# Turning normalised FFN tokens with a DMA transpose on SyncE's queue in place of TensorE transposes

## The reference, cut to what matters

```
x = x + _L0_ffn_ref(_layernorm(x, axis=-1), W_up, W_gate, W_down)

def _L0_ffn_ref(x, W_up, W_gate, W_down):
    wu, wg, wd = ternary_quant(W_up), ternary_quant(W_gate), ternary_quant(W_down)
    up = jnp.einsum('bsd,ed->bse', x, wu)        # D = 512, FF = 2048
    gate = jnp.einsum('bsd,ed->bse', x, wg)
    hidden = jax.nn.silu(up) * gate
    return jnp.einsum('bse,de->bsd', hidden, wd)
```

## Time and profile before

| what | value |
|---|---|
| median of 3 executions | 768.12 us (767.45 to 768.91) |
| span of the profiled execution, first to last instruction | 762.1 us |
| what lies around the span, by the median | 6.0 us |
| PE busy over the span | 718.1 us, 94% |
| DVE / ACT / POOL busy | 51% / 36% / 14% |
| mean granted TensorE clock | 0.983 |

### The profile page before, as it was taken

The page is one execution under the profiler, slowest core; times in us unless marked ns, Lnnn a source line. Parts: engine busy times, 40 slices in busy tenths (PEclk is TensorE's granted clock), DMA queues, the critical chain, the costliest instruction groups (busy, mean ns, idle before and its releaser), DMA issues.

```text
span 762.1 us, 11832 instructions
## 1 busy us (share of the span) xinstructions
PE 718.1 (94%) x3882; PEld 380.7 (50%) x3883; DVE 388.6 (51%) x672; ACT 276.1 (36%) x430; POOL 108.5 (14%) x154
## 2 busy tenths in 40 slices
PE   4999999999996789999994999999999999999997
PEld 2465556566464556555553444444444444444443
DVE  5568666676537855444457343453434434343223
ACT  3465554555454355222224222222222222222221
POOL 4203034033021400000005000000000000000000
PEclk9999999999998999999997999999999999999999
DMA  7983034033044396222212000020000100010001
GB/s 223 391 320 143 1 127 151 0 129 147 1 173 159 130 342 232 78 91 83 83 42 70 27 15 14 14 71 14 15 0 14 69 14 14 0 55 1 0 0 55
DMA packets 32493, 66.73 MB, mean 88 GB/s; under 512 B 6352, under 2 KB 6352, under 8 KB 31440
## 3 DMA queue, kind: packets, MB, share of 16 engines
q1 hardware_dynamic: 28464, 53.24, 20.1%
q0 software_dynamic: 4000, 13.11, 5.0%
HBM read 47.73 MB, written 18.61 MB: 87 GB/s over the span
## 4 chain that ended last, share of the span: by engine, by line
PE 85%; DVE 5%; DMA 3%; issue 2%; ACT 2%; POOL 2%; SPq 1%; DVEq 0%; POOLq 0%; ACTq 0%
PE bank L1056 31%; PE bank L1314 29%; PE bank L1324 14%; PE bank L1049 6%; PE bank L1199 2%; PE bank L1213 1%; DMA nrm<-in_L_ffn_W_down_dram 1%; PE bank L1234 1%; DMA stage<-in_L_attn_Wv_dram 1%; DVE w_att L843 1%; DVE w_att L842 1%; SPq L183 1%; POOL rs L305 1%; DVE st L568 1%; DMA n<-sorted_outputs,pos_now 0%
## 5 line engine op out<-in xcount | busy, mean ns | idle before, releaser
L1314 PE MATMUL bank<-w_att,region 128*128 128x512 f16 (+1 forms) x1024 | 233.1, 381 | 0.8 <-ACT w_att L535 0.8
L1314 PEld LDWEIGHTS bank<-w_att,region 128*128 (+1 forms) x1024 | 100.5, 98 | 120.5 <-issue 3.6
L1022 DVE SCALAR_TENSOR_TENSOR tmp<-tmp,hk,bank 128x512 f32<-128x512 f32 x64 | 47.8, 747 | 153.7 <-PE bank L1314 153.3
L1324 PE MATMUL bank<-region,tmpA 128*128 (+1 forms) x504 | 119.1, 379 | 0.0
L1056 PE MATMUL bank<-w_moe,tmpA 128*128 x456 | 104.6, 379 | 1.5 <-DVE tmpA L913 1.5
L1056 PE MATMUL bank<-xT,w_att 128*128 128x512 f16 x384 | 88.6, 387 | 4.3 <-DVE region L753 2.3
L543 ACT ACTIVATE tmp<-bank,qs 128x512 f32<-128x512 f32 x64 | 44.0, 688 | 125.1 <-PE bank L1314 125.1
L547 ACT ACTIVATE tmpA<-tmp 128x512 f16<-128x512 f32 x64 | 40.4, 631 | 121.7 <-DVE tmp L1022 121.7
L1324 PEld LDWEIGHTS bank<-region,tmpA 128*128 128x128 f16 x504 | 49.2, 98 | 59.6 <-DVE stage L1005 0.9
L1056 PEld LDWEIGHTS bank<-w_moe,tmpA 128*128 128x128 f16 x456 | 44.4, 98 | 47.1 <-issue 1.7
L1025 DVE TENSOR_TENSOR tmpA<-tmp,tmpA 128x512 f16<-128x512 f32 x64 | 44.3, 692 | 45.7 <-ACT tmpA L547 45.7
(11 more groups left out here) (134 smaller groups left out, 752.4 us busy)
## 6 DMA issues: line engine op xcount, KB each, us to landing
stage<-in_L_ffn_W_up_dram SPq DMA_DIRECT2D x8, 1024.0 KB
stage<-in_L_ffn_W_gate_dram SPq DMA_DIRECT2D x8, 1024.0 KB, 7.0
sorted_tokens<-a SPq DMA_DIRECT2D x10, 512.0 KB, 10.3
n<-sorted_tokens SPq DMA_DIRECT2D x20, 256.0 KB, 2.6
stage<-in_ctx_dram SPq DMA_DIRECT2D x4, 1024.0 KB
stage<-in_L_ffn_W_down_dram SPq DMA_DIRECT2D x4, 1024.0 KB
nrm<-in_L_ffn_W_down_dram SPq DMA_DIRECT2D x4, 1024.0 KB, 7.4
out_dram<-stage SPq DMA_DIRECT2D x16, 256.0 KB, 2.1
```

The source lines that it names most:

```text
L1022: dve.scalar_tensor_tensor(out=h32, in0=sil, scalar=hk[:, 0:1], in1=gate_ps[:, :], op0=ALU.mult, op1=ALU.mult).then_inc(s["hid_mul"], 1)
L1314: mm = pe.matmul(dst, w[:, bass.ds(cf_c, 1), k * P:(k + 1) * P].rearrange("p a n -> p (a n)"), x3T[:, bass.ds(b, 1), i, k].rearrange("p a ...
L1324: mm = pe.matmul(ffy_ps[t][:, :], hid[:, parity, i, t * P:(t + 1) * P], tern[2][:, bass.ds(c, 1)].rearrange("p a n -> p (a n)"), start=(st ...
```

## The change

For batches 1 to 3 the tile is no longer turned by PE. ACT and DVE split the normalised tile into its two fp16 halves as it lies, tokens on partitions, into `x3h`, a buffer of 128 x 1024 fp16 that takes the place of `nrm[:, 1]`, which is free by then. One DMA transpose on SP's queue for each tile then turns both halves at once, SBUF to SBUF, 256 KB, into `x3T`. PE's wait at the start of a batch is on these DMAs. SP's order of work is written out: the four transposes of batch 1, then the stores of a batch and the transposes of the batch two later. The next tile's split waits until the DMA before it has read `x3h`. Batch 0 stays as it was.

```
+    x3h = nrm[:, 1].bitcast(F16).rearrange("p (i d) -> p i d", i=2)
...
-        with sp.Fori(0, B) as b:
+        def x3_turned(b):
+            for t in range(T):
+                sp.wait_ge(s["x3_lo"], T * b + t + 1)
+                sp.dma_start_transpose(
+                    out=x3T[:, bass.ds(b, 1), :, :, t * P:(t + 1) * P].rearrange("p a i k s -> p (a i k) s"),
+                    in_=x3h.rearrange("p i d -> p (i d)")).then_inc(s["x3_in"], 16)
+
+        def stored(b):
             for t in range(T):
                 sp.wait_ge(s["out_made"], T * b + t + 1)
                 sp.dma_start(out_v[:, bass.ds(T * b + t, 1)].rearrange("p a d -> p (a d)"), out_slot[t]).then_inc(
                     s[f"out_done{t}"], 16)
+
+        x3_turned(1)
+        with sp.Fori(0, B - 2) as b:
+            stored(b)
+            x3_turned(b + 2)
+        stored(B - 2)
+        stored(B - 1)
...
+        def x3_hi_rows(i):
+            act.wait_ge(s["x3_norm"], i + 1)
+            act.wait_ge(s["x3_in"], 16 * (i - T))
+            act.activation(x3h[:, 0], nrm[:, 0], ACT.Copy).then_inc(s["x3_hi"], 1)
...
                 if nxt and cc == 2:
-                    x3_hi(b + 1, t)
+                    x3_hi_rows(T * (b + 1) + t)
...
+        def x3_lo_rows(i):
+            dve.wait_ge(s["x3_hi"], i + 1)
+            dve.tensor_tensor(x3h[:, 1], nrm[:, 0], x3h[:, 0], ALU.subtract).then_inc(s["x3_lo"], 1)
...
         def x3_normalise(b, t):
             i = T * b + t
             dve.wait_ge(s["rs3"], 2 * (i - T) + 2)
-            dve.wait_ge(s["t3_mm"], i)
+            dve.wait_ge(s["x3_lo"], i)
+            dve.wait_ge(s["t3_mm"], T)
...
                 if nxt and cc == 2:
-                    x3_lo(b + 1, t)
+                    x3_lo_rows(T * (b + 1) + t)
...
-                if nxt and cc == 1:
-                    x3_transpose((b + 1) * T + t, 0, t3_ps)
...
             if not first:
-                pe.wait_ge(s["x3_lo"], T * b + T)
+                pe.wait_ge(s["x3_in"], 16 * T * b)
```

More of the change, by code:

```diff
@@ L145, in decoder @@
     z_ps, y_ps, tx_ps, th_ps, q_ps = ps[0], ps[1], ps[2], ps[3], ps[4:8]
-    ffy_ps, up_ps, gate_ps, t3_ps = ps[0:4], ps[4], ps[5], ps[6]
+    ffy_ps, up_ps, gate_ps = ps[0:4], ps[4], ps[5]
     names = """x_first0 x_first1 x_first2 x_first3 x_rest cols_in rows_in tok_in att_in0 att_in1 att_in2
@@ L159, in decoder @@
         tx_mm xs_hi xs_lo z_mm z_act h_mul th_mm h_hi h_lo y_mm y_evac sign_a sign_b unit_mm unit_copy
-        y_added x3_stat x3_aggr x3_norm t3_mm x3_hi x3_lo pos3_copied
+        y_added x3_stat x3_aggr x3_norm t3_mm x3_hi x3_lo x3_in pos3_copied
         up_mm gate_mm up_act hid_mul hid_hi hid_lo down_mm down_last out_made""".split()
@@ L530, in _, with x3_hi @@
             unit_copies(3, j)
[L533 to L536, removed]
+        def x3_hi(t, bank):
+            act.wait_ge(s["t3_mm"], t + 1)
+            act.activation(x3T[:, 0, 0, :, t * P:(t + 1) * P], bank[:, :].rearrange("p (k s) -> p k s", k=K),
+                           ACT.Copy).then_inc(s["x3_hi"], 1)
+        def x3_hi_rows(i):
+            act.wait_ge(s["x3_norm"], i + 1)
+            act.wait_ge(s["x3_in"], 16 * (i - T))
+            act.activation(x3h[:, 0], nrm[:, 0], ACT.Copy).then_inc(s["x3_hi"], 1)
         def group(b, t, first, nxt):
@@ L548, in group @@
                 if nxt and cc == 2:
-                    x3_hi(b + 1, t)
+                    x3_hi_rows(T * (b + 1) + t)
         for t in range(T):
-            x3_hi(0, t, ps[t])
+            x3_hi(t, ps[t])
         def batch3(b, first, nxt):
@@ L931, in _, with x3_lo @@
         signs_of(3, 2)
[L934 to L938, removed]
+        def x3_lo(t, bank):
+            dve.wait_ge(s["x3_hi"], t + 1)
+            hi, lo = (x3T[:, 0, i, :, t * P:(t + 1) * P] for i in range(2))
             dve.tensor_tensor(lo, bank[:, :].rearrange("p (k s) -> p k s", k=K), hi, ALU.subtract).then_inc(s["x3_lo"], 1)
+        def x3_lo_rows(i):
+            dve.wait_ge(s["x3_hi"], i + 1)
+            dve.tensor_tensor(x3h[:, 1], nrm[:, 0], x3h[:, 0], ALU.subtract).then_inc(s["x3_lo"], 1)
         def sum3(t):
@@ L975, in _ @@
         for t in range(T):
-            x3_lo(0, t, ps[t])
+            x3_lo(t, ps[t])
         def x3_sum(b, t):
@@ L1299, in _, with x3_transpose @@
             unit_transposes(3, j)
[L1302 to L1305, removed]
+        def x3_transpose(t, bank):
+            pe.wait_ge(s["x3_norm"], t + 1)
             transposes(bank, lambda k: nrm[:, t, k * P:(k + 1) * P]).then_inc(s["t3_mm"], 1)
@@ L1346, in group @@
                     down(cf - 1, c - 1, (cc - 1) % 2, begins and cc == 1, False)
-                if nxt and cc == 1:
-                    x3_transpose((b + 1) * T + t, 0, t3_ps)
         for t in range(T):
-            x3_transpose(t, t, ps[t])
+            x3_transpose(t, ps[t])
         pe.wait_ge(s["unit_copy"], 12 * T)
```

## The result

The changed kernel runs in 761.35 us, the median of six executions (760.32 to 762.63), against 767.79 for six of the kernel before: ratio 0.9934, 95% interval 0.9913 to 0.9954. It is faster by 0.66%; the two medians alone, 6.4 us apart, would make a ratio of 0.9916, which lies inside the interval. The forecast was 770.9 us, slower by 0.36%, with a range from 762.8 to 790.0: sign and range both missed. What came true is the rival "hidden, or nearly", which had 0.38.

A forecast was written before the change was run, and what follows sets the result against it. PE was taken as the bound, without gaps in the FFN stage. Removing transposes gave -5.3 us, three boundary waits of 6.0 - 3.3 us gave +8.1, together +2.8: 770.9 us against the median of 768.12, range 762.8 to 790.

The forecast's parts named there:

- hidden, or nearly: Rival at the starts of batches 1 to 3: the transfer takes under 4.6 us, kernel faster, 762.8 us if fully covered; chance 0.38.
- the price of the turned transfer: DMA transpose of one 256 KB tile on SP's queue: 6.0 us from issue to landing, range 2.1 to 10.4.
- the three boundary terms: At the starts of batches 1 to 3, PE waits d - 3.3 us each; 8.1 us in all at d = 6.0.
- the cover: From last low half to PE's first load of the next batch: 3.53 us, 3.3 left for the transfer after issue and wake.
- What is removed: FFN stage, batches 1 to 3: 12 sets of four PE transposes at 0.44 us each, 5.3 us off the chain.
- What is changed at nothing: Split in the FFN stage: ACT's cast from SBUF 0.05 us longer, DVE's low half 0.69 us, new waits delaying nobody.
- SP's queue: Transposes placed ahead of and behind the result stores: a few us more in the queue cost nothing, late stores not missed.
- The sum's form: Whole change: -5.3 us plus three times the landing time beyond 3.3 us; +2.8 us at 6.0, break-even at 5.1.
- When a stall takes the clock: Rival at batch starts: landing 7.3 us or more, stall over 4 us, about 3 us of work lost each; chance 0.17.
- My forecast's own case: At batch starts, PE late by 1.3 to 4 us each, landing 4.6 to 7.3 us, time 766.6 to 774.8 us; chance 0.40.
- What lies around the span: Outside the profiled span of the whole kernel: 6.0 us added to the 764.9 us span to give the forecast time.
- the hidden case: At batch starts, landing within 3.3 us, so no PE wait and 5.3 us gained: 762.8 us, the range's low end.

## Why the prediction was wrong

The step that failed is **the price of the turned transfer**. I took d = 6.0 us from issue to landing, because the tokens' load (4.8 us) and 1.9 us for the bytes seemed the nearest rows, and kept 2.1 as the floor. It is 3.0. The loads of tokens and columns move single 4-byte elements at the start of the kernel, with megabytes of other loads in flight; the transpose goes in 256-byte pieces through idle DMA engines. Which of the two differences makes those loads slower was not tried. The rows nearer to it were the ones that I used as floor and as an argument for the rival: the store of as many bytes (2.1) and above all the gather (3.4). The same DMA view of before also has 20 plain loads of 256 KB on SP's queue (`n<-sorted_tokens`) that land after 2.6 us, which the earlier trace rows leave out. Turning as such adds 0.1 us to a copy of the same pieces.

With d = 3.0 in the prediction's own sum, d - 3.3 is below zero, the three boundary terms vanish and -5.3 us is left. The size was wrong, and with it the sign; that the transfer counts only by what it exceeds the cover was right.

- **What is removed**: right. 12 x 0.44 = 5.3 forecast; putting the transposes back lengthens the stage from 324.9 (324.6 where nothing is turned) to 329.8 us and brings the time back to that of before.
- **What is changed at nothing**: right. ACT 0.61 us, DVE 0.68, and what follows them starts as before. That the new wait of ACT costs nothing follows from the transfers' 3.0 us in a distance of 20.7.
- **The cover**: right in kind, small in size. 3.3 us forecast; SP issues 0.03 to 0.13 us after the low half instead of 0.17, and 3.6 to 3.7 us are there. With d of 3.9 us PE stood for 0.16 us, with 4.5 for 0.7.
- **SP's queue**: right. The stores still land after 2.1 us, and no engine waited for them.
- **The sum's form** held where it was tried. A wait is the landing less the cover: 2.4 to 2.7 us forecast for four transposes a tile and 2.31 to 2.71 measured, 4.7 forecast for the split in cc = 3 and 4.30 to 5.26 measured. The waits and the slower matmuls behind them give the longer stage within 0.3 us in three versions. No single transfer of 6 us was tried; the late landings were made with more issues or a later split.
- **When a stall takes the clock**: I had it from 4 us on. At 4.3 us and more it did each time, by 1.5 to 2.7 us for a stall, where I had put 3; but it also did after 2.31 us, in one case of three of about that length. My forecast's own case could have cost more than the +2.8 us that I gave it, as the four transposes a tile did: the sum had no term for the clock below d = 7.3.
- **What lies around the span** was not 6.0 us. In all executions that have both, time and span differ by 1.6 to 1.7 us. By that, the profiled execution of before took about 763.8 us (an estimate, 762.1 + 1.7), and the median of 768.12 belonged to others. That didn't bear on the difference, but 762.8 as the time of the hidden case, the low end of the range, was taken from the median of three, without room for the spread of medians: those of before were 768.12, 767.79, 766.88, 765.49 and 767.37 us. With d of 3.0 the sum gives 762.8; that 761.35 was measured is less than this spread away.
- **A slip without weight**: in the second half of the page's PE slices two are below 9 tenths, a 4 and the last one's 7, not one.

On the two rules of the Trainium skill: "Advanced Engine Details and Errata", X-Bar Transpose (TRN2), has transposes as fast as plain DMAs, and the landing times of 3.0 us for the transpose and 2.9 for a plain copy of the same pieces agree; what the prediction put in for a plain DMA, the store's 2.1, was not that copy. The figure of 1309 ns for a 128x128 block, in "VectorE: DVE Perf Modes", The three transpose paths, is near what one block as its own DMA holds the queue for here, 1.14 us in the median. Multiplying it by eight, as the prediction tried, comes near only where eight are issued: 10.02 us for a tile.

## What to carry to other kernels

An operation that is moved from the bound engine to an idle DMA queue is worth its full time there if its last instance lands before it is wanted: measure the cover at the boundary, and give it a whole step of slack more where that costs nothing. Turn many blocks with one DMA, because the issue costs nearly the same for one block (1.14 us) as for eight (1.23). And price an unseen transfer by the rows with the same bytes in a quiet stage (here 2.1, 2.6 and 3.4 us, around the 3.0 measured), not by a row that only shares the name of the difficulty. Last, leave a margin for the clock: a short stall of PE can cost more than its length (2.31 us of waiting took 1.7 us more here).

## What the runs showed of the hardware that was not expected

**A DMA transpose's issue has nearly one price.** It holds SP's queue for 1.23 us with eight blocks of 128x128, 1.19 with four, 1.17 with two and 1.14 in the median with one, against 0.62 us for a plain copy of the same 256 KB. The landing falls with size, but not in proportion: 3.0, 2.4 and 2.3 us after the issue for 256, 128 and 64 KB.

**A transfer now and then lands late, mostly with an instruction packet ahead of its bytes.** In most traces one tile's transfer does. The DMA view of the changed kernel from 584.3 to 588.3 us, in 40 slices of 0.1 us, has the last transpose of batch 2:

```profile
GB/s 0 0 0 0 0 0 0 0 0 0 164 26 154 205 218 195 212 179 82 23 0 8 8 10 8 10 10 10 28 266 287 289 292 104 0 0 0 0 0 0
...
q8 instruction: 1, 0.02, 1.7%
...
w_att<-nrm SPq DMA_TRANSPOSE x1, 3.9
```

One packet of the instruction queue, 0.02 MB, is in this window, and a burst stands just ahead of the transpose's data. The transpose then moves at some 200 GB/s, falls to about 10 for some 0.9 us, and ends at near 290. The window of the transpose at 501.3 us has no such packet and no hole, and it lands after 3.0 us:

```profile
GB/s 0 0 0 0 0 0 0 0 0 0 0 3 115 225 223 218 218 207 223 200 207 212 200 190 147 36 0 0 0 0 0 0 0 0 0 0 0 0 0 0
```

The packet of that queue was there too with the transposes that took 4.5 us in the second trace of the changed kernel, 4.4 in the second trace of the split in cc = 1 and 4.0 with two transposes a tile, and with the one plain copy of 12 that took 3.6 instead of 2.9. With TensorE's transposes put back no such packet falls into a transpose, and all land after 3.0 to 3.1 us. But it is not the only thing that makes a landing late: the transpose issued at 503.88 with the split in cc = 3 took 3.9 us with no packet of that queue beside it and no hole, its bytes through by 506.5 us and its landing at 507.8. That the fetch is the cause in the other cases is read from these coincidences; no experiment tried it, and what held up that other landing is open.

**The clock after a wait of about 2.4 us is not settled.** It fell after 2.31 us and stayed after 2.44 and 2.71, in the same trace. What else it hung on is left open.
